# The head of a hybrid attention kernel: one transfer for the projection matrix, the weight folds in a row, the first batch in two token halves, and the rounding of the down matrix moved into the attention loop

## What is computed

```python
x = x + attn(layernorm(x))      # layernorm again inside, then q, k, v, causal softmax, out @ o_proj, + its own input
x = x + ffn(layernorm(x))       # silu(h @ gate * gs) * (h @ up * us) @ down * ds, weights rounded to fp8 e4m3
x = x + s4d(layernorm(x))       # convolution along the time axis (here 2 steps: one tap and one lag tap) + x * D
x = x + ffn(layernorm(x))       # the same weights
```

## Time and profile before

| | |
|---|---|
| median of 3 runs | 127.56 us (127.39 to 127.65) |
| the profiled execution | 127.35 us, of which the span from first to last instruction 125.6 us |
| busy: PE, DVE, POOL, ACT | 116.5, 94.4, 86.8, 77.6 us |
| granted TensorE clock | 1.00 over the whole span |
| first matrix transpose of real data | 4.98 us |
| attention loop ends, feed-forward begins | 52.45 us |

### The profile page before, as it was taken

How to read it: one execution, slowest core, us unless ns; L and a number is a source line. 1 busy time by engine, 2 the same in 40 slices (tenths; PEclk the granted TensorE clock), 3 DMA queues, 4 the chain that set the end, 5 groups by cost and what they waited for, 6 DMA issues and landing times.

```text
span 125.6 us, 2089 instructions
## 1 busy us (share of the span) xinstructions
PE 116.5 (93%) x666; PEld 77.3 (62%) x666; DVE 94.4 (75%) x226; ACT 77.6 (62%) x147; POOL 86.8 (69%) x168
## 2 busy tenths in 40 slices
PE   5997999999999999999999999989999869999970
PEld 5885468658668758745769545567446457556640
DVE  0398999919865866949797899947899946784592
ACT  2145079695875468858865278865578764579800
POOL 2246469999999888888433578889978870038831
PEclk9999999999999999999999999999999999999999
DMA  3998940000000000000000000000000000000404
GB/s 90 297 277 322 354 135 8 0 0 0 0 0 0 5 5 0 0 0 0 0 0 5 0 0 0 0 3 5 0 0 0 3 0 0 5 0 24 143 0 167
DMA packets 5682, 5.80 MB, mean 46 GB/s; under 512 B 1140, under 2 KB 5160, under 8 KB 5672
## 3 DMA queue, kind: packets, MB, share of 16 engines
q1 hardware_dynamic: 4648, 5.52, 13.3%
q10 hardware_dynamic: 960, 0.15, 0.7%
q0 software_dynamic: 64, 0.02, 0.1%
HBM read 4.63 MB, written 1.05 MB: 45 GB/s over the span
## 4 chain that ended last, share of the span: by engine, by line
PE 66%; DVE 11%; POOL 10%; ACT 4%; issue 3%; DMA 3%; SPq 0%; POOLq 0%; DVEq 0%; ACTq 0%
PE psum L1195 22%; PE psum L1211 10%; PE psum L1134 7%; PE psum L1109 7%; PE psum L1074 6%; POOL rstd L296 4%; DMA qkv_sb<-in_qkv 3%; PE psum L1067 3%; DVE stats L696 3%; PE psum L1156 2%; PE psum L1122 2%; POOL f_tail L451 2%; ACT h_rows L559 2%; ACT normed L529 2%; PE psum L1050 2%
## 5 line engine op out<-in xcount | busy, mean ns | idle before, releaser
L607 ACT ACTIVATE gated<-psum,scales 128x512 f32<-128x512 f32 x24 | 16.3, 681 | 13.1 <-PE psum L1195 13.1
L451 POOL TENSOR_TENSOR f_tail<-fused,f_head 128x512 f16<-128x512 f32 x12 | 14.1, 1173 | 12.8 <-ACT f_head L613 12.5
L1211 PE MATMUL psum<-down,f_head 128*128 128x256 bf16 x96 | 22.1, 273 | 0.5 <-POOL f_tail L451 0.5
L1211 PE MATMUL psum<-down,f_tail 128*128 128x256 bf16 x96 | 22.0, 272 | 0.0
L958 DVE SCALAR_TENSOR_TENSOR fused<-psum,up_scales_fit,gated 128x512 f32<-128x512 f32 (+1 forms) x25 | 17.8, 716 | 4.6 <-PE psum L1195 3.3
L613 ACT ACTIVATE f_head<-fused 128x512 f16<-128x512 f32 (+1 forms) x25 | 15.1, 606 | 3.4 <-DVE fused L958 3.2
L966 DVE TENSOR_TENSOR f_tail<-fused,f_head 128x512 f16<-128x512 f32 (+1 forms) x13 | 9.7, 749 | 9.2 <-ACT f_head L613 9.1
L1195 PE MATMUL psum<-h_head,up 128*128 128x512 f16 x48 | 14.3, 379 | 0.0
L1195 PE MATMUL psum<-h_tail,up 128*128 128x512 f16 x48 | 14.3, 379 | 0.0
L1195 PE MATMUL psum<-h_tail,gate 128*128 128x512 f16 x48 | 14.3, 379 | 0.0
L1195 PE MATMUL psum<-h_head,gate 128*128 128x512 f16 x48 | 14.3, 379 | 0.0
(11 more groups left out here) (167 smaller groups left out, 257.2 us busy)
## 6 DMA issues: line engine op xcount, KB each, us to landing
x_in<-in_x SPq DMA_DIRECT2D x4, 256.0 KB, 4.2
qkv_sb<-in_qkv SPq DMA_DIRECT2D x3, 256.0 KB, 4.0
gate_raw<-in_gate_w SPq DMA_DIRECT2D x1, 768.0 KB, 6.8
up_raw<-in_up_w SPq DMA_DIRECT2D x1, 768.0 KB, 8.6
down_raw<-in_down_w SPq DMA_DIRECT2D x1, 768.0 KB, 10.3
out<-x_in SPq DMA_DIRECT2D x3, 256.0 KB, 2.1
wo_sb<-in_o_proj SPq DMA_DIRECT2D x1, 256.0 KB, 5.3
down_scale_all<-in_down_scale SPq DMA_DIRECT2D x1, 128.0 KB, 10.1
```

Source lines behind the costliest of these rows:

```text
L451: pool.tensor_tensor(f_tail[:, m, :], fused[:, m % FUSED, :], f_head[:, m, :], ALU.subtract).then_inc(f_tail_by_pool, 1)
L607: act.activation(gated[:, m % 2, :], psum[:, BANK_GATE[m % 2], :], ACT.Silu, scale=gate_scales[:, m:m + 1]).then_inc(gated_ready, 1)
L1211: last = pe.matmul(down_columns(n, t), part[:, m, t * P:t * P + P], down16[:, m, :], start=(m == 0 and (t % 2 == 0 or n == 2 * B - 1) and ...
```

## The change

- SP loads the whole `qkv` (256 rows of 768 values) in one transfer behind the first piece of x, and `o_proj` before the second half of x. Gamma, beta and D come by ACT's queue, ahead of the three small loads that stood there; `log_dt` is no longer part of `param_rows`. C_re and C_im, which POOL loaded, come by SP behind the down matrix.
- PE warms up 17 times in one go, then turns q, k and v in a row and does both folds before `g`. `g` and `v` of the first batch are made in halves of 256 tokens, and `scores(0)` and `scores(1)` come before the second half of `g`.
- DVE copies the turned k matrix (ACT copied all three), and its statistics of tiles 2 to 7 stand behind that copy. POOL makes the scales of x + layernorm(x) ahead of the rounding of the gate matrix.
- DVE's part in the down matrix is placed into the attention loop: `grid_end(2)` after `attention_out(0)`, `magnitude` and the first lift after `attention_out(2)`, the second lift and the first lowering after `attention_out(3)`, the second lowering after `attention_out(4)`.

Three operations of 768 columns have come in, two ahead of `row_max(6)` and one ahead of `row_max(7)`. The diff, cut to its core:

```diff
-WARM_UP = 14
-WARM_BETWEEN = 8
+WARM_UP = 17
...
-        BANK_WT, BANK_WQK, BANK_WVO, BANK_PARAMS, BANK_SCALES, BANK_NORMS = [4, 5, 3], 2, 3, 7, 4, 5
+        BANK_WT, BANK_WQK, BANK_WVO, BANK_PARAMS, BANK_SCALES, BANK_NORMS = [4, 5, 3], 2, 4, 7, 4, 5
-        BANK_G = [[6, 7], [0, 1]]
+        BANK_G = [[5, 2], [0, 1]]
...
             load_x(0)
-            load_chunks(qkv_sb[:, :, 0:KEY], qkv[:, 0:KEY], q_loaded)
+            load_chunks(qkv_sb[:], qkv, qkv_loaded)
             load_x(1)
-            load_chunks(qkv_sb[:, :, KEY:2 * KEY], qkv[:, KEY:2 * KEY], k_loaded)
-            load_rows(param_rows, (gamma, beta, log_dt, d_param), params_loaded)
-            load_chunks(qkv_sb[:, :, 2 * KEY:], qkv[:, 2 * KEY:], v_loaded)
+            load_chunks(wo_sb[:], o_proj, wo_loaded)
             load_x(2)
             load_x(3)
-            load_chunks(wo_sb[:], o_proj, wo_loaded)
...
+            for n, array in ((2, c_re), (3, c_im)):
+                load_chunks(s4d_in[:, n, :].rearrange("p (c n) -> p c n", c=C), array, c_loaded)
...
+            x_plus_scales()
             round_weight(0, gate16, gate_up_ready)
-            x_plus_scales()
...
             turned(0)
-            turned(1)
+            turned(2)
+            xn_half(0)
+            act.wait_ge(wqk_made, 1)
+            act.activation(wqk[:].rearrange("p c n -> p (c n)"), psum[:, BANK_WQK, :], ACT.Copy).then_inc(wqk_ready, 1)
+            act.wait_ge(wvo_made, 1)
+            act.activation(wvo[:].rearrange("p c n -> p (c n)"), psum[:, BANK_WVO, :], ACT.Copy).then_inc(wvo_ready, 1)
+            g_first_half()
             act.wait_ge(tanh_in, 1)
...
+            xn_half(1)
             for k in range(T, K):
...
-            g_part(0)
-            xn_chunk(1)
+            v_part(0)
...
             first_stats(0)
             normalise((0, 1))
+            copy_params()
+            copy_k()
+            xn_half(0)
             first_stats(2)
+            first_stats(T)
+            normalise((2, 3))
+            first_stats(T + 2)
             exp_reduce()
-            normalise((2, 3))
...
+            xn_half(1)
             exp_finish()
...
             grid_end(0)
-            g_chunk(0)
+            row_max(0)
+            row_max(1)
+            g_second_half()
+            xn_second()
+            v_half(0)
             grid_begin(1)
-            xn_chunk(1)
             grid_end(1)
             grid_begin(2)
-            v_half(0)
-            row_max(0)
-            grid_end(2)
-            row_max(1)
-            lift_down(0)
-            g_chunk(1)
-            lift_down(1)
-            lower_down(0)
+            g_chunk()
             v_half(1)
...
                 attention_out(k - 2)
+                if k == 2:
+                    grid_end(2)
                 if k == 4:
+                    magnitude()
+                    lift_down(0)
+                if k == 5:
+                    lift_down(1)
+                    lower_down(0)
+                if k == 6:
                     lower_down(1)
-                    magnitude()
...
-            turn_w(0, q_loaded)
-            warm_up(WARM_BETWEEN)
-            turn_w(1, k_loaded)
+            turn_w(0)
+            turn_w(1)
+            turn_w(2)
...
+            turn_z_half(0)
+            pe.wait_ge(q_v_turned, 1)
+            pe.wait_ge(k_turned, 1)
             fold(BANK_WQK, 0, lambda kc: w_turned[:, 1, kc, :]).then_inc(wqk_made, 1)
-            turn_z(0, (2, 3))
-            turn_w(2, v_loaded)
-            pe.wait_ge(wqk_ready, 1)
-            pe.wait_ge(params_ready, 1)
-            make_g(0)
...
             fold(BANK_WVO, 2, lambda kc: wo_sb[:, kc, :]).then_inc(wvo_made, 1)
+            pe.wait_ge(wqk_ready, 1)
+            make_g_half(0)
+            turn_z_half(1)
+            pe.wait_ge(wvo_ready, 1)
+            make_v(0, (0, 1))
...
-            turn_z(1)
-            pe.wait_ge(wvo_ready, 1)
-            make_v(0)
             scores(0)
+            scores(1)
+            pe.wait_ge(v_by_act, 1)
+            make_g_half(1)
+            turn_z()
+            make_v(0, (2, 3))
+            columns_there(3)
```

More of the change, by code:

```diff
@@ L108, in hybrid_layer @@
         pos_half = sb("pos_half", [P, M])
-        param_rows = sb("param_rows", [4 * C, P])
-        params = sb("params", [P, 4 * C])
-        gammas, betas, log_dts, d_params = (params[:, C * n:C * n + C] for n in range(4))
+        param_rows = sb("param_rows", [3 * C, P])
+        params = sb("params", [P, 3 * C])
+        gammas, betas, d_params = (params[:, C * n:C * n + C] for n in range(3))
         scale_rows = sb("scale_rows", [2 * M, P])
@@ L511, in v_part @@
                                ACT.Copy).then_inc(v_by_act, 1)
+            load_row(0, gamma)
+            load_row(1, beta)
+            load_row(2, d_param)
             act.dma_start(e_in[:, 0:HN].rearrange("p (c n) -> p c n", c=C),
@@ L584, in _ @@
             exp_scores(0)
-            g_part(1)
+            exp_scores(1)
+            g_part()
             square_weights(1)
-            exp_scores(1)
             copy_probs(0)
@@ L1052, in fold, with turn_z, turn_z_half, columns_there @@
                 return last
-            def turn_z(b, tiles=range(T)):
-                for t in tiles:
-                    pe.wait_ge(z_by_act if b else z_ready, t + 1)
+            def turn_z():
+                for t in range(T):
+                    pe.wait_ge(z_by_act, t + 1)
                     for c in range(C):
-                        turned = pe.transpose(column(BANK_Z[b][c], t * P, P), normed[:, T * b + t, c * P:c * P + P], ident[:])
+                        turned = pe.transpose(column(BANK_Z[1][c], t * P, P), normed[:, T + t, c * P:c * P + P], ident[:])
                         if t == T - 1:
                             turned.then_inc(z_turned, 1)
-            def make_g(b):
-                pe.wait_ge(xn_by_act, b + 1)
-                pe.wait_ge(xn_by_dve, b + 1)
+            def turn_z_half(half):
+                for t in (2 * half, 2 * half + 1):
+                    pe.wait_ge(z_ready, t + 1)
+                    for c in range(C):
+                        last = pe.transpose(column(BANK_Z[0][c], t * P, P),
+                                            normed[:, t, c * P:c * P + P], ident[:])
+                last.then_inc(z_turned, 1)
+            def columns_there(made):
+                pe.wait_ge(xn_by_act, made)
+                pe.wait_ge(xn_by_dve, made)
+            def make_g_half(half):
+                columns_there(half + 1)
                 for j in range(C):
                     for c in range(C):
-                        last = pe.matmul(column(BANK_G[b][j], 0, S), wqk[:, c, j * P:j * P + P], xn_cols[:, b, c, :],
+                        last = pe.matmul(column(BANK_G[0][half], j * (S // 2), S // 2), wqk[:, c, j * P:j * P + P],
+                                         xn_cols[:, 0, c, HALVES[half]], start=(c == 0), stop=(c == C - 1))
+                last.then_inc(g_made, 1)
+            def make_g():
+                for j in range(C):
+                    for c in range(C):
+                        last = pe.matmul(column(BANK_G[1][j], 0, S), wqk[:, c, j * P:j * P + P], xn_cols[:, 1, c, :],
                                          start=(c == 0), stop=(c == C - 1))
                     last.then_inc(g_made, 1)
-            def make_v(b):
-                for t in range(T):
+            def make_v(b, tiles=range(T)):
+                for t in tiles:
                     for c in range(C):
```

93 lines of the change are left out of this document (50 added, 43 removed).

## The result

The changed kernel takes 128.15 us (median of 8 runs, 127.98 to 128.93) against 127.34 for the kernel before on the same chip (8 runs, 126.99 to 127.65): a ratio of 1.0087, 95% interval 1.0063 to 1.0111. It is slower by 0.8 us. The forecast was 129.8, slower by 2.2: the right direction, but a size beyond the lower end of the range (128.2).

What follows compares the result with a forecast made beforehand. PE was taken to bound the kernel; a head lead of 0.6 us against loop costs of 0.67 and 2.16 gave +2.2 us, from 127.56 to 129.8 us. The whole range was 128.2 to 131.2.

Steps and rivals of the forecast that it cites:

- What bounds it: Whole kernel: PE, followed almost without a hole from 19.10 to beyond 70 us; DVE work costs only where PE waits.
- The head: From the loads to `turn_probs(0)`: PE gets there at 27.4 instead of 28.03 us, a lead of 0.6 us.
- the landing: Start of the head: the single projection transfer lands at 6.2 us, bounds 5.9 and 8.3.
- the wait for v: In the head: PE stands about 0.75 us before the second half of g, until ACT's copy of v frees a bank.
- PE's steps: In the head: PE's work counted forward with earlier durations, such as 1.3 us for 12 transposes and 1.86 per fold.
- better head: Rival, 15%: PE's two waits shrink and the transfer lands sooner, lead 1.5, `grid_end(2)` takes 0.96: 128.6 us.
- third term: In the 128.6 us sum: the 2.16 us added for lifts and lowerings ahead of `row_max(6)` and `row_max(7)`.
- The grid step: `grid_end(2)` after `attention_out(0)`: makes `row_max(3)` 0.67 us late, all reaching PE at `attend(2)`; bounds 0.36 and 1.43.
- The rounding ahead of `row_max(6)` and `row_max(7)`: Late loop: lifts and lowerings make these 1.8 and 2.24 us late; 2.16 us reach PE at tile 7's probabilities.
- The sum: Whole kernel: -0.6 + 0.67 + 2.16 = +2.2 us, 129.8 us against the median of 127.56.
- The loop hides it: Rival, 8%: DVE's spare time in the loop absorbs the added rounding and the head's lead stays: 127.0 us.
- The slow head: Rival, 12%: PE idles after warm-up and the slow pace holds through 12 transposes and the first fold: 131.3 us.

Runs made afterwards that it cites:

- e2: Kernel before, with only the rounding of the down matrix moved into the attention loop as the change does: 129.66 us, ratio 1.0199.
- e3: Changed kernel without the two lifts and two lowerings (down matrix unrounded, grid steps kept): 126.98 us, ratio 0.9982.
- e5: Changed kernel with the second lowering after `attention_out(5)` instead of after `attention_out(4)`: 128.54 us, ratio 1.0096.
- e4_no_grid: Changed kernel without lifts, lowerings and `grid_end(2)` (down matrix unrounded): 125.97 us, ratio 0.9894.
- e11: Changed kernel with the projection matrix loaded in three transfers (q, k, v) instead of one: 131.01 us, ratio 1.0251.
- e1: Changed kernel with the down matrix's rounding back at its old places, mostly ahead of the loop: 132.94 us, ratio 1.0422.
- e13: v_first plus second lowering after `attention_out(5)`, POOL's middle taps before its lowering wait, DVE's down-matrix reduction in the second feed-forward pass: 127.35 us.
- e15: e13 with DVE's reduction over the up matrix also moved, to the third feed-forward pass: 127.38 us, ratio 1.0007.
- e18: e13 with 20 warm-up matmuls instead of 17: 127.36 us.
- v_first: Changed kernel with ACT's copy of v of the first half ahead of the second batch's four normalised rows: 126.94 us, ratio 0.9988.
- e6: Changed kernel with the five down-matrix steps, `grid_end(2)`, lifts and lowerings, spread over other gaps: 127.65 us, ratio 1.0028.
- e16: e1 with POOL's scales of x back behind its rounding of the gate matrix: 130.47 us, ratio 1.0265.

## Why the prediction came out too slow

- *What bounds it.* Right. PE is followed through the loop, and added DVE work shows where PE waits, at `attend(2)`, `attend(5)` and tile 7's probabilities, as forecast.
- *The head.* This step failed first and most. The lead was put at 0.6 us. In the profile it is 1.03, but this execution had the late piece of x. By the medians, which set the changed kernel against the same loop with the old head, it is 129.66 - 128.15 = 1.5 (by the ratios, 1.4), and the old head of e2 ran 0.37 ahead of the kernel before itself: 1.9 against that kernel. By the distances of the other five profiles (17.33 us from the first fold to tile 0's probabilities) it is 27.87 - (8.45 + 17.33) = 2.1 at the profile's fast transposes, and 1.4 to 1.5 in e3 and e5, where they took 2.0 to 2.1 us. That is the end of the text's own bounds (2.1 without waits, landing at 5.9). Three terms were mis-sized: the landing, 6.2 forecast and 5.7 measured (0.5); the wait for v, 0.75 forecast and 0.2 without the late piece (0.55), mainly because from POOL's start to ACT's first row were 2.14 us in e5 (13.52 to 15.66) and not 2.66; and PE's steps, some 0.4 shorter in sum than counted. The "better head" rival, with 15%, had a lead of 1.5 and gave 128.6, the nearest of all; but its grid step of 0.96 us did not come with it, and its third term was 0.55 too large, so that its number is in part luck.
- *The grid step.* Forecast 0.67, measured 0.78 in the changed kernel's profile (1.62 us long instead of 1.27), 1.07 with the old head (1.90) and 1.14 in e5 (1.97). The range of 0.36 to 1.43 held, the middle was too low. The Trainium skill's rule in SBUF — State Buffer, Who interferes with whom, that VectorE and GpSimd exclude each other for a whole instruction, agrees in kind with what the runs show: the step takes 1.03 or 1.97, and which of the two is settled by 0.3 us of phase.
- *The rounding ahead of `row_max(6)` and `row_max(7)`.* This step failed too. Forecast 2.16, measured 1.61 in the changed kernel and 1.60 with the old head. I added full durations and handoffs, 1.95 + 0.09 and 1.04 + 0.06; from start to start they take 1.84 and 0.85. `row_max(7)` came 1.37 late, with a lead of 0.25 left at `attend(2)`: 1.62 and not 2.24. Of that 0.6, 0.20 + 0.25 are these two; the other 0.17 are the two handoffs ahead of them, which overlap too (the lift starts at 43.72, the aggregate before it ends at 43.80).
- *The sum.* With the measured terms -1.03 + 0.78 + 1.61 = +1.4 in the profile, against +2.2. The other 0.6 is the profiled execution's distance from the median. The late piece of x cost it 18.39 - 17.33 = 1.06 us in the head, of which the grid step gave back 10.68 - 10.32 = 0.36. Without both it would have taken 128.74 - 0.70 = 128.04 us; four of the eight runs lie at 127.98 to 128.09. This is an estimate from the other profiles: no profile of the changed kernel shows such an execution, so it is argued, not shown. In its terms the change comes to -2.1 + 1.1 + 1.6 = +0.6 with fast transposes, and measured is +0.8. Against the absolute forecast, 129.8, another 0.2 is the kernel before, which took 127.34 us in this series and not 127.56.
- *The rivals.* "The loop hides it" is refuted by e2_loop_alone, +2.5, and by the rows: no idle time of DVE is left ahead of `row_max(3)`, `row_max(6)` and `row_max(7)`. "The slow head" does occur (e4_no_grid's profiled execution, e11), but not in most executions. Half of it is more frequent: twelve transposes took 2.0 us or more in the profiles of e1, e3, e5, e13, e15 and e18 too, but the folds behind them ran at the fast pace (1.96 or 1.97 us for eight matmuls, as in the changed kernel), so the price of slow folds, up to 132.0 us, was not paid.
- *What the text did not ask*: what the old places of the rounding would cost under the new head. With e1_head_alone at +5.8 the two halves of the change can't be priced apart: their single effects, +5.8 and +2.5, do not add up to +0.8.

## What to carry to other kernels

Price a step that is inserted in a chain by the distance from start to start of such steps in the trace, not by its duration and a handoff. Where two engines exclude each other, what counts is who comes first: before moving a big VectorE step, list GpSimd's big steps at the new time, and give it two prices. Before a wait in one profile is taken for the program's, look at what stands at its start: here it was one late transfer, and the same code in five other profiles waited 0.2 us. And when a chain is made shorter and nothing comes out, look for the engine that fed on the old delay; here there were GpSimd, VectorE and ScalarE in a row behind it. Freeing the first two was worth 0.1 us, while one copy put ahead of four (v_first) was worth 1.2, of which 0.95 came from the turn that another step got by it.

## What the hardware showed that I had not expected

- The third piece of x, 256 KB, landed 8.5 us after issue in one execution, and DVE stood 1.55 us for it; in the profiles of e1, e3, e5, e6 and e16, with the same order of loads, DVE did not wait for it.
- One transfer of 768 KB landed 4.4 us after issue; split into three, with v issued directly behind k, the pieces took 3.2 to 5.8 us, and k came at 7.7 instead of 5.7.
- The load of `c_re`, 256 rows of 32 bytes, held SyncE's queue for 4.09 us in the changed kernel's profile (2.60 in e5_last_later, 1.77 in e11_three_pieces).
- The granted clock read 1.00 all the while that 12 equal transposes took from 1.53 to 2.82 us. The Trainium skill, TensorE: Matmul & The Clock Gate, Part 4: PE-mode transpose, has it that transposes do not count as busy for the clock; here the trace differs: 1.53 us for twelve is 0.13 each, against 0.23 in the warm-up, and PE had run nothing but transposes before.
